# A gated attention layer on one core: decay sums from a tile mixed by two copies

## The reference

```
q, k = swish(x Wq), swish(x Wk);  v = x Wv
g = log_sigmoid(x Wf) / 8;        s = 1 - exp(g)
for each token t:                 # h_k and h_v are 64x64 states
    h_k = h_k * exp(g_t)[None, :] + k_t[:, None] * s_t[None, :]
    p   = softmax(q_t / 8 @ h_k)
    h_v = h_v * exp(g_t)[:, None] + s_t[:, None] * v_t[None, :]
    o_t = p @ h_v
out = (o / rms(o) * g_norm_w) @ Wo
```

## Time and profile before

| | |
|---|---|
| median of 3 runs | 3343.43 us |
| profiled execution | 3342.4 us, of it span from first to last instruction 3340.7 us |
| attention phase | from about 1432 to 2370 us of the span |
| TensorE busy over the span | 3139.5 us (94%) |
| VectorE / ScalarE / GpSimd busy | 2628.2 (79%) / 1611.2 (48%) / 1292.9 us (39%) |
| transfers on SyncE's queue, share of 16 DMA engines | 29.8% |

### The profile page before, as it was taken

The page is one execution under the profiler, slowest core; times in us unless marked ns, Lnnn a source line. Parts: engine busy times, 40 slices in busy tenths (PEclk is TensorE's granted clock), DMA queues, the critical chain, the costliest instruction groups (busy, mean ns, idle before and its releaser), DMA issues. The chain is left out here.

```text
span 3340.7 us, 101263 instructions
## 1 busy us (share of the span) xinstructions
PE 3139.5 (94%) x36224; PEld 2699.3 (81%) x36224; DVE 2628.2 (79%) x4369; ACT 1611.2 (48%) x4426; POOL 1292.9 (39%) x2170
## 2 busy tenths in 40 slices
PE   5999999999988999979999999999799999999999
PEld 4888888888875655668888888888688888888888
DVE  7999999999973333258888888888699999999998
ACT  3333333333325555567777777777333333333332
POOL 3333333333324333335555555555333333333332
PEclk9999999999999999989999999999899999999999
DMA  3111111111115555534444444444211111111111
GB/s 86 54 56 52 52 53 55 52 52 54 55 45 184 196 196 197 196 118 128 128 129 131 125 129 132 126 129 126 64 57 52 52 55 53 52 53 55 52 52 47
DMA packets 294595, 307.33 MB, mean 92 GB/s; under 512 B 95092, under 2 KB 261364, under 8 KB 294520
## 3 DMA queue, kind: packets, MB, share of 16 engines
q1 hardware_dynamic: 294520, 306.31, 29.8%
HBM read 171.97 MB, written 117.44 MB: 87 GB/s over the span
## 5 line engine op out<-in xcount | busy, mean ns | idle before, releaser
L580 PE MATMUL mid_ps<-xT_hl,w_hl 128*128 128x128 f16 x12288 | 728.1, 219 | 0.0
L427 PE MATMUL res_ps<-w_hl,midT_hl 128*128 128x256 f16 x6144 | 712.5, 273 | 1.2 <-DVE x_out L548 1.2
L580 PEld LDWEIGHTS mid_ps<-xT_hl,w_hl 128*128 128x128 f16 x12288 | 697.3, 98 | 0.5
L384 POOL TENSOR_TENSOR var_eps<-moments,eps_col 128x1 f32<-128x1 f32 x384 | 110.1, 287 | 1478.6 <-DVE moments L380 1478.6
L427 PEld LDWEIGHTS res_ps<-w_hl,midT_hl 128*128 128x128 f16 x6144 | 589.4, 98 | 65.6 <-DVE midT_hl L535 1.7
L488 ACT ACTIVATE midT_hl<-mid_ps 128x1024 f16<-128x1024 f32 x256 | 262.2, 1024 | 692.3 <-PE mid_ps L591 692.3
L514 DVE TENSOR_TENSOR_SCAN runmax<-restart,logits_ps 128x1024 f32<-128x1024 f32 x256 | 581.2, 2270 | 4.0 <-PE logits_ps L569 3.8
L399 ACT ACTIVATE xn_hl<-xc,rstd 128x256 f16<-128x256 f32 x384 | 194.2, 506 | 436.2 <-POOL rstd L389 347.2
L374 DVE BATCH_NORM_STATS2 stats<-x_in 128x6 f32<-128x256 f32 x384 | 161.7, 421 | 293.2 <-DMA x_in<-x 288.7
L535 DVE SCALAR_TENSOR_TENSOR midT_hl<-mid_ps,midT_hl 128x1024 f16<-128x1024 f32 x256 | 313.5, 1225 | 15.4 <-ACT midT_hl L488 7.5
L519 DVE TENSOR_TENSOR step<-runmax 128x1024 bf16<-128x1024 f32 x256 | 314.8, 1230 | 7.9
(11 more groups left out here) (140 smaller groups left out, 6044.0 us busy)
## 6 DMA issues: line engine op xcount, KB each, us to landing
projected<-qkfv_out SPq DMA_DIRECT2D x128, 512.0 KB, 2.9
qkv<-projected SPq DMA_DIRECT2D x128, 384.0 KB, 3.4
x<-x_out SPq DMA_DIRECT2D x256, 128.0 KB, 1.8
x_in<-x SPq DMA_DIRECT2D x256, 128.0 KB, 2.1
x_res<-x SPq DMA_DIRECT2D x256, 128.0 KB, 2.1
x_in<-in_L_attn_x SPq DMA_DIRECT2D x128, 128.0 KB, 2.1
x_res<-in_L_attn_x SPq DMA_DIRECT2D x128, 128.0 KB, 2.1
gate<-projected SPq DMA_DIRECT2D x128, 128.0 KB, 3.1
```

The source lines that it names most:

```text
L427: last = nc.tensor.matmul(dst, left(lp, k), right(rp, k), start=(k == 0 and lp == rp), stop=(k == blocks - 1 and lp == 1))
L580: nc.tensor.matmul(mid_ps[t.slot][:, cols], w1_hl[:, wp, k, cols], xT_hl[:, t.ring, xp, k], start=(c % PER_BANK == 0 and k == 0 and wp == xp),
```

## The change

A new float16 tile `gate_mix` (4 buffers, as `gate_hl`) is filled by two transfers on SyncE's queue, one for rows 0 to 63 from this tile's gates and one for rows 64 to 127 from the last tile's. The decay sums then take one product per part, with a matrix of GATE in every place (`each16`), in place of two with the two half-filled ones. `each16` is made by one memset in place of two tensor_scalar instructions in the set-up. The transfers are a new stage `mix_gates` with offset 3, the first in SyncE's list, for chunks 1 to 3; it waits for `gate_low` of its tile. TensorE waits for both transfers, between the `G_ps` products and the decay products. Eight semaphores are added.

```
-        late16 = sb("late16", [P, P], f16)
-        early16 = sb("early16", [P, P], f16)
+        each16 = sb("each16", [P, P], f16)
...
-                    nc.gpsimd.tensor_scalar(early16[:, :], half_f[:, :], GATE, None, ALU.mult)
-                    nc.gpsimd.tensor_scalar(late16[:, :], half_f[:, :], -GATE, GATE, ALU.mult, ALU.add)
+                    nc.gpsimd.memset(each16[:, :], GATE)
...
+            gate_mix = fb("gate_mix", [P, 4, 2, D], f16)
...
+            now_mixed, past_mixed = four("now_mixed"), four("past_mixed")
...
+                    def mix_gates(t):
+                        if t.chunk:
+                            after(sp, S["gate_low"], t)
+                            sp.dma_start(gate_mix[0:MIDDLE, t.ring], gate_hl[0:MIDDLE, t.ring]
+                                         ).then_inc(now_mixed[t.ring], 16)
+                            sp.dma_start(gate_mix[MIDDLE:P, t.ring], gate_hl[MIDDLE:P, (t.ring - 1) % 4]
+                                         ).then_inc(past_mixed[t.ring], 16)
...
-                    pipeline(sp, [(load_residual, -3), (load_qkv, 2), (load_gate, 6), (store, -4), (turn_o, -2)],
+                    pipeline(sp, [(mix_gates, 3), (load_residual, -3), (load_qkv, 2), (load_gate, 6), (store, -4), (turn_o, -2)],
...
-                        past = gate_hl[:, (t.ring - 1) % 4]
+                        mix = gate_mix[:, t.ring]
...
-                            terms = [(late16, past), (early16, now)]
-                            for n, (ones, gates) in enumerate(terms):
-                                for part in range(2):
-                                    last = nc.tensor.matmul(decay_ps, ones[:, :], gates[:, part],
-                                                            start=(n == 0 and part == 0), stop=(n == 1 and part == 1))
+                            after_ring_dma(pe, now_mixed, t)
+                            after_ring_dma(pe, past_mixed, t)
+                            for part in range(2):
+                                last = nc.tensor.matmul(decay_ps, each16[:, :], mix[:, part],
+                                                        start=(part == 0), stop=(part == 1))
...
-                                for n, (ones, gates) in enumerate(terms):
-                                    for part in range(2):
-                                        last = nc.tensor.matmul(col_ps[:, a:a + 1],
-                                                                gates[:, part, a * P:(a + 1) * P], ones[:, 0:1],
...
+                                for part in range(2):
+                                    last = nc.tensor.matmul(col_ps[:, a:a + 1], mix[:, part, a * P:(a + 1) * P],
+                                                            each16[:, 0:1], start=(part == 0), stop=(part == 1))
```

More of the change, by code:

```diff
@@ L1203, in log_gate_sums @@
                             for a in range(PAIRS):
-                                for n, (ones, gates) in enumerate(terms):
-                                    for part in range(2):
-                                        last = nc.tensor.matmul(col_ps[:, a:a + 1],
-                                                                gates[:, part, a * P:(a + 1) * P], ones[:, 0:1],
-                                                                start=(n == 0 and part == 0),
-                                                                stop=(n == 1 and part == 1))
+                                for part in range(2):
+                                    last = nc.tensor.matmul(col_ps[:, a:a + 1], mix[:, part, a * P:(a + 1) * P],
+                                                            each16[:, 0:1], start=(part == 0), stop=(part == 1))
                             last.then_inc(S["decay_col_done"], 1)
```

## The result

The changed kernel takes 3358.81 us (median of 6 runs, 3356.27 to 3360.49), the one before 3344.26 us in the same runs: a ratio of 1.0043, 95% interval 1.0030 to 1.0056. It is slower by some 14.5 us. The forecast was 3344.5 us, the range ended at 3356; the rival "qkv comes late" had 3355 to 3366.

The account below looks back on a forecast made before the run. The prediction took a loop through TensorE, VectorE and ScalarE as the bound. Products, waits and loads at 0 and +1.1 us at the start made 3343.5 us, 3344.5 us as a median; range 3336 to 3356 us.

Parts of the forecast that it names:

- qkv comes late: Added issues and bytes delay qkv loads, so k's transposes on the loop wait: 3355 to 3366 us, chance 0.11.
- Products removed: On TensorE, 0.32 us less per tile of chunks 1 to 3, beside the loop: taken as 0.
- the tie of 0.09 us: In the chunk 3 step, TensorE's own work and x_out end together to within 0.09 us; gain 0 to 2.9 us.
- The 30.7 us that a TensorE-bound phase would give: If TensorE bounds every step, all removed products count: 30.7 us off, to 3314 us, chance 0.04.
- Waits on TensorE: Two added waits before the decay products find their copies already landed: taken as 0, at most 0.28 us.
- Transfers on SyncE's queue: Two copies issued ahead of the loads delay qkv within its margins: cost 0, at the upper ends 21 us.
- The shift: How far the copies move qkv's load back: 0.9 us for issues and wait, 1.0 us with bytes, at most 1.84.
- The margin: Time from qkv's landing to k's transposes at 1818.18: 1.39 us, the smaller of two margins.
- The bound of 0.65 us a cycle: Upper-end loss from late qkv: 0.45 us past the first margin and 0.20 past the second, 21 us in all.
- The bytes: The copies' 128 KB ahead of qkv on the DMA engines: 0 to 0.46 us, taken as 0.1.
- The start: At the phase's start, tile 0's qkv load goes out behind the first copies, once: +1.1 us.
- The signs: Profile checks: cycle still 28.56 us; wrong if over 0.2 us away, and if longer, look for a cause in the loads.

Follow-up runs that it names:

- The halved products alone: Changed kernel without copies or waits, decay sums taken from this tile's gates with the full matrix: 3346.07 us, ratio 1.0001 against the kernel before.
- the copies alone: Changed kernel's two copies and their waits, with all products as in the kernel before and the mixed tile unused: 3354.61 us, ratio 1.0031.
- the small copies alone: Kernel before plus the two copies and their waits, each copy cut to 32 bytes per row (2 KB), all products kept: 3355.78 us, ratio 1.0032.

## Why the prediction was wrong

*Products removed, taken as 0: right.* The halved products alone have a ratio of 1.0001. For the step of chunk 3 I named x_out as what would hold it; the runs show another wait beside it, read_out's for the masked products. That one stands before the transposes, so the saving is used up before x_out is asked for, and the tie of 0.09 us that I weighed was never reached. My sign that x_out would be waited for in every step (84 of 84) did not come: 61 of 83. The 30.7 us that a TensorE-bound phase would give were sized right, 27.4 us where it is TensorE-bound.

*Waits on TensorE, taken as 0: right.* Copies behind the loads, with both waits, cost nothing that can be measured.

*Transfers on SyncE's queue, taken as 0: this is the step that failed.* Two of its terms were mis-sized, and both the same way; together they made the cost 0. The shift: I took 0.9 us out of 0.80 to 1.38, by the row where the transposing transfer follows a store after 0.40 us, on the argument that the copies have fixed addresses. The measured shift is 1.26 us (1.28 in the median). In the changed kernel a copy takes 0.48 to 0.60 us on the queue, median 0.59, and with 2 KB a copy the figures are the same. I had only one row for a short issue, and it showed how soon something may follow a store, not how long an SBUF-to-SBUF copy issues. The margin: I took 1.39 us from one step, as all the time from the load's landing to k's transposes. Two things were wrong in that. Over 26 cycles of the kernel before (tiles 16 to 120) this margin runs from 0.91 to 1.56 us, median 1.18, since the loads in question land in 3.0 to 3.7 us after their issue. And not all of it can be used: where the load is what holds them, k's transposes start 0.22 us behind its landing, in 24 of 26 cycles of the changed kernel to within 0.01 us. That leaves 0.96 us, and already the shift of 1.0 us that I forecast would have used it up. 1.28 - 0.96 = 0.32 us is an estimate of the cost from these rows; the step of chunk 3 grew by 0.31 us. The bound of 0.65 us a cycle held.

*The bytes:* 0.1 us taken, and the copies of 2 KB and of 64 KB cost alike. The Trainium skill, "SBUF — State Buffer", section "Door 1: The DMA port swizzle (why `[64,N]` ≈ `[32,N]`)", had made the pair 0.60 us of transfer, as an estimate, and 3.5 us in all. That was nearer to the result than my 0, but by luck: the loss came from the issues, and copies of one thirty-second of the bytes lose as much. No run here shows the ports' rate alone.

*The start, taken as +1.1 us: about right, in part by luck.* k's first transposes came 2.0 us later by the load, where the sum had 1.2 to 1.6: the two copies held the queue from 1440.31 to 1441.52, 1.21 us and not 0.80. Some 0.8 us was made up by tile 4.

*The signs.* The cycle is 28.88 us, over 0.2 from 28.56, and the cause was where I had said to look, in the loads.

*The rival* of a late qkv had the mechanism, the place and the sign. Its price at half the bound, 10 us, and at the bound, 21 us, stand on either side of the 14.5 us measured. By the rival's own term, 32 cycles of 0.31 us, it is 9.9 us; the rest lies in the start of the phase and in the long waits and the clock of the first 16 tiles. I gave it 0.11 and should have seen that of the two ends of the shift the one I took rested on a different kind of transfer. It was to decide from a shift of 1.39 us; it did from 0.96. What stays open is why the copies alone come out at 10 us by their ratio and the changed kernel at 14. The profiles place part of the difference: between tiles 16 and 120 the copies alone lose 5.3 us and the changed kernel 8.0, with the loads issued in the step of chunk 3 landing after 3.31 and 3.38 us on average; one execution of each cannot say whether that is the kernels or chance. Open, too, is whether the fall of the clock near 1540 us is in every execution of the changed kernel.

## What to carry to other kernels

An engine at 94% busy need not be the bound: removing work from TensorE gave 0 here, and 27.4 us once VectorE's list and the transfer queue let go of the loop. A transfer that is itself harmless has a price on its queue, 0.6 us an issue here, and pays it in whatever stands behind it; put it behind the transfers that the loop waits for. A margin has to be taken from the spread of landings, and not from one step, and less what passes between a landing and the work that waited for it, 0.22 us here: with 0.96 us of margin left and a shift of 1.0 to 1.84, the forecast should have been "slower". A late load can also cost more than its delay: at an idle time of 1.74 us the granted clock fell to 0.50 and stayed there for 6.9 us.

## What the runs showed of the hardware

From 1500 to 2100 us an SBUF-to-SBUF copy on SyncE's queue holds it for 0.48 to 0.60 us (0.61 at 2 KB), median 0.59, with consecutive issues 0.53 to 0.63 us apart, median 0.62, both at 64 KB and at 2 KB. In the kernel before, a load holds it for 0.33 to 0.42 us in the median and qkv's issue follows the residual's after 0.59 to 0.69; a transposing transfer holds it for 1.20 (median) and follows a store after 0.39 to 0.41. The landings from 1500 to 2100 us (count, KB each, median us to landing), of the changed kernel and of the small copies alone:

```profile
gate_mix<-gate_hl SPq DMA_DIRECT2D x124, 64.0 KB, 2.0
```

```profile
gate_mix<-gate_hl SPq DMA_DIRECT2D x124, 2.0 KB, 1.8
```

Thirty-two times the bytes cost 0.2 us of landing and nothing of issue.
